# Film block: 21 of the 100 lags of a causal convolution moved to TensorE, the other 79 on VectorE in two halves in turns

## The reference, cut to what matters

```
x = layernorm(x_text, g_norm_in, b_norm_in)
scale_in, shift_in = jnp.split(c_t @ W_film_in + b_film_in, 2, axis=-1)
x = x * (1.0 + mod_gate * scale_in) + mod_gate * shift_in
y = s4d(x, ...)          # y[:, t] = sum over j <= t of K[:, j] * x[:, t - j], plus x * D_skip
scale_out, shift_out = jnp.split(c_t @ W_film_out + b_film_out, 2, axis=-1)
y = y * (1.0 + mod_gate * scale_out) + mod_gate * shift_out
xt = x_text + y
h = layernorm(xt, g_ffn, b_ffn)
```

## Time and profile before

| | us |
|---|---|
| three runs | 5372.17, 5390.11 (median), 5404.51 |
| profiled execution: its time | 5378.79 |
| profiled execution: its span | 5376.5 |
| busy PE / PEld / DVE / ACT / POOL | 4182.6 / 2777.6 / 3022.1 / 2105.8 / 1545.1 |
| L2454, 100 lags: first start, last end | 4848.9, 4969.6 |
| mean granted clock of TensorE | 0.83 of 2.4 GHz |

### The profile page before, as it was taken

How to read it: one execution, slowest core, us unless ns; L and a number is a source line. 1 busy time by engine, 2 the same in 40 slices (tenths; PEclk the granted TensorE clock), 3 DMA queues, 4 the chain that set the end, 5 groups by cost and what they waited for, 6 DMA issues and landing times. The chain is left out here.

```text
span 5376.5 us, 84862 instructions
## 1 busy us (share of the span) xinstructions
PE 4182.6 (78%) x25870; PEld 2777.6 (52%) x25870; DVE 3022.1 (56%) x4511; ACT 2105.8 (39%) x3190; POOL 1545.1 (29%) x911
## 2 busy tenths in 40 slices
PE   7899999999989887578889999983844344340799
PEld 4588888888745456434445555541522222220455
DVE  3344444454333333345456666557369999968333
ACT  2255555555512231124334544441335555530122
POOL 1266666666500031004310000000325555530000
PEclk8799999999979987689779999786866565655699
DMA  2000000000011103120022222210000000000011
GB/s 81 1 9 18 18 12 15 18 18 18 1 34 50 32 9 84 30 68 2 1 54 62 59 59 61 49 26 0 1 23 25 17 25 25 17 10 0 4 56 44
DMA packets 124597, 152.67 MB, mean 28 GB/s; under 512 B 86912, under 2 KB 110224, under 8 KB 124080
## 3 DMA queue, kind: packets, MB, share of 16 engines
q1 hardware_dynamic: 124208, 147.72, 11.0%
HBM read 109.43 MB, written 2.66 MB: 21 GB/s over the span
## 5 line engine op out<-in xcount | busy, mean ns | idle before, releaser
L980 POOL TENSOR_TENSOR pexp_lo<-arena,pexp_hi 128x800 fp32r<-128x800 f32 x384 | 637.4, 1660 | 434.4 <-POOLq L979 433.1
L2123 DVE TENSOR_REDUCE arena<-ps 100x1 f32<-100x482 f32 (+1 forms) x768 | 490.1, 658 | 270.0 <-DVEq L2110 256.9
L2003 DVE TENSOR_REDUCE arena<-ps 128x1 f32<-128x482 f32 (+3 forms) x624 | 393.2, 657 | 361.1 <-DVEq L1981 347.2
L1287 ACT ACTIVATE arena<-ps 128x800 f32<-128x800 f32 x384 | 322.4, 840 | 495.4 <-ACTq L1285 493.4
L2421 DVE MATCH_REPLACE8 arena<-arena 100x1444 f32<-100x1444 f32 x256 | 421.3, 1660 | 0.0
L3140 PE MATMUL ps<-kst,qs 96*100 96x482 f32 (+1 forms) x768 | 378.3, 495 | 45.7 <-PEq L3094 42.0
L1377 ACT ACTIVATE arena<-ps 128x800 f32<-128x800 f32 x384 | 315.3, 837 | 244.5 <-ACTq L1376 244.0
L926 POOL TENSOR_TENSOR max_diag<-w_const,arena 100x800 fp32r<-100x800 f32 x160 | 247.0, 1543 | 451.9 <-POOLq L924 451.9
L2512 DVE TENSOR_TENSOR arena<-ps,arena 128x400 f32<-128x400 f32 x256 | 147.2, 575 | 339.3 <-DVEq L2511 339.3
L3269 PE MATMUL ps<-w_const,w_cross 100*128 100x100 f32 x192 | 43.2, 380 | 375.4 <-PEq L3266 375.4
L1288 ACT ACTIVATE pexp_hi<-ps 128x800 fp32r<-128x800 f32 x384 | 319.5, 832 | 0.0
(11 more groups left out here) (372 smaller groups left out, 9196.6 us busy)
## 6 DMA issues: line engine op xcount, KB each, us to landing
ctxT<-in_ctxT SPq DMA_DIRECT2D x59, 541.5 KB
kst<-mid SPq DMA_DIRECT2D x128, 180.5 KB, 3.1
ctxk<-in_ctx SPq DMA_DIRECT2D x43, 528.0 KB
chunk<-in_ff_chunks SPq DMA_DIRECT2D x77, 193.0 KB, 2.4
arena<-gate_dram SPq DMA_DIRECT2D x64, 200.0 KB, 3.8
kst<-xn SPq DMA_DIRECT2D x64, 180.5 KB, 2.9
arena<-gate_dram SPq DMA_DIRECT2D x64, 100.0 KB, 2.6
w_cross<-in_ca SPq DMA_DIRECT2D x1, 3728.5 KB, 12.3
```

Of the source, the lines that this page charges most:

```text
L980: own(nc.gpsimd.tensor_tensor(pexp_lo[p % 3][:, :, :], pexp[p % 3], pexp_hi[p % 3][:, :, :], ALU.subtract))
L1287: nc.scalar.activation(pexp[p % 3], of, ACT.Exp, scale=scale).then_inc(s.pexp_ready, 1)
L2003: peak = nc.vector.tensor_reduce(mparts[0:at.stop - at.start, m, c:c + 1], bank(k, z - a, at.stop - at.start), AX.X, ALU.max)
L2123: peak = nc.vector.tensor_reduce(mparts2[:, h, c:c + 1], bank(k, z - a, S), AX.X, ALU.max)
```

## The change

In the film block TensorE computes lags 0 to 20 of the convolution. For each of them ScalarE makes a diagonal matrix once, identity times the column of `kernel_l`, in a new tile `lag_diag` in the arena; these 21 instructions stand between `batch(B - 1, 1, last=True)` and `scale(1, 1)`. After `modulate("film_in")` TensorE waits for VectorE's `stage_pe` and adds up 21 products for each group in bank 4 + g, ahead of `modulate("film_out")` in its order. VectorE does the skip and lags 21 to 99, each in two halves of eight batches in turns with a semaphore for each half, then adds the four banks to `y`.

```
@@ setup @@
+    PE_LAGS = 21
+    lag_diag = shared([128, PE_LAGS, 128])
@@ ScalarE, film_block @@
             batch(B - 1, 1, last=True)
+            for j in range(PE_LAGS):
+                ins = nc.scalar.activation(lag_diag[:, j, :], W("const", "ident"), ACT.Copy, scale=kernel_l[:, j:j + 1])
+            own(ins)
+            act.sem_inc(s.k_diag_ready, 1)
             scale(1, 1)
@@ VectorE, film_block @@
             modulate("film_in", xn)
+            dve.sem_inc(s.stage_pe, 1)
             y = squares
-            nc.vector.tensor_scalar(y[:, :, :], xn[:, :, :], W("tk", "skip"), None, ALU.mult).then_inc(s.dve_done, 1)
-            dve.wait_ge(s.dve_done, 1)
-            dve.sem_inc(s.dve_done, -1)
-            for j in range(S):
-                nc.vector.scalar_tensor_tensor(y[:, :, j:S], xn[:, :, 0:S - j], kernel_l[:, j:j + 1], y[:, :, j:S],
-                                               ALU.mult, ALU.add).then_inc(s.dve_done, 1)
+            halves = [slice(0, B // 2), slice(B // 2, B)]
+            for i, h in enumerate(halves):
+                nc.vector.tensor_scalar(y[:, h, :], xn[:, h, :], W("tk", "skip"), None, ALU.mult).then_inc(done[i], 1)
+            for j in range(PE_LAGS, S):
+                for i, h in enumerate(halves):
+                    finished(i)
+                    nc.vector.scalar_tensor_tensor(y[:, h, j:S], xn[:, h, 0:S - j], kernel_l[:, j:j + 1], y[:, h, j:S],
+                                                   ALU.mult, ALU.add).then_inc(done[i], 1)
+            finished(0)
+            finished(1)
+            for g in range(NG):
+                dve.wait_ge(s.film_full, 1)
+                dve.sem_inc(s.film_full, -1)
+                nc.vector.tensor_tensor(group(y, g), group(y, g), bs(bank(4 + g)), ALU.add).then_inc(s.dve_done, 1)
                 dve.wait_ge(s.dve_done, 1)
                 dve.sem_inc(s.dve_done, -1)
             modulate("film_out", y)
@@ TensorE, film_block @@
             modulate("film_in")
+            pe.wait_ge(s.stage_pe, 1)
+            pe.sem_inc(s.stage_pe, -1)
+            pe.wait_ge(s.k_diag_ready, 1)
+            pe.sem_inc(s.k_diag_ready, -1)
+            for g in range(NG):
+                for j in range(PE_LAGS):
+                    ins = mm(bs(bank(4 + g))[:, :, j:S], lag_diag[:, j, :], xn[:, GB * g:GB * g + GB, 0:S - j],
+                             start=j == 0, stop=j == PE_LAGS - 1, skip_group_check=True)
+                ins.then_inc(s.film_full, 1)
             modulate("film_out")
```

## The result

| | before | after |
|---|---|---|
| median of four executions | 5384.51 us | 5325.74 us |
| lowest, highest | 5372.17, 5404.51 | 5303.69, 5339.99 |
| profiled execution, its time | 5378.79 | 5339.99 |
| its span | 5376.5 | 5338.2 |

The ratio is 0.9884, with a 95% interval of 0.9836 to 0.9932: faster, by 0.7 to 1.6%. (It is the ratio of the means of the four; that of the medians is 0.9891.) Of the repetitions used further down, e1's 5375.71 and 5435.35 and e4's 5927.30 count as slow, being over 1.5% above the fastest execution of their kernel, and all ratios leave them out. I had said 5346, with 5326 to 5372 for 8 in 10. The median is 0.3 us under that range, so the range was wrong, and the question is why. The profiled execution, at 5339.99, is the slowest of the four.

A forecast was written before the change was run, and what follows sets the result against it. VectorE was taken to bound the convolution while TensorE idles. Saving 42.3 us and losing 2.3 gave -40.0, from 5378.79 to 5338.8, carried to the level of four executions, 7.6 higher: 5346 us, with 5326 to 5372 for 8 in 10.

The forecast's parts named there:

- lags 21 to 99 in halves: VectorE's convolution: 158 half lags, each overlapping the one before by 0.09 us, take 74.9 us.
- stretch saved: Convolution on VectorE, skip to film_out: film_out starts at 4927.5 instead of 4969.8, 42.3 us saved.
- TensorE's 168 instructions: Lags 0 to 20 on TensorE: 84 products of two instructions, 30,240 columns, 50.4 us at 2.4 GHz.
- diagonals at the end of the attention: ScalarE ahead of `scale(1, 1)`: 21 diagonals take 6.1 us, so GpSimd starts its sums 2.3 us late.
- B: Rival, VectorE's lags: halves don't overlap, 88.9 us in place of 74.9, time 5360 us; chance 0.13.
- C: Rival, VectorE's lags: each half costs as much as a lag now, 111.0 us, time 5382 us; chance 0.03.
- right on the full level, and leave no gap: TensorE's new products start at 4847.9 at the full clock and end at 4898.3, 25 us of slack.
- D: Rival, convolution: TensorE at 1.2 GHz throughout, its products take 100.8 us, time 5370 us; chance 0.06.
- E: Rival, convolution: TensorE's weight loads aren't hidden, its products take 158 us and bound the kernel, 5428 us; chance 0.04.
- The end moves by the same: End of the attention: GpSimd's two sums keep their 3.58 us, so the end shifts by the 2.3 us delay.
- term added for the level: Whole time: the profiled execution is 7.6 us below the mean of four, 5386.4, so the sum is carried to 5346.
- a dear ScalarE: End of the attention, bound for the diagonals: at 0.52 us each, 10.9 us, they cost 7.1 us.

The follow-up runs named there:

- e1: The changed kernel run again, unedited: median 5347.04 us of 12 executions, ratio 0.9900 to the kernel before.
- e4: The changed kernel with the 21 diagonals behind `scale(1, 1)` instead of ahead of it: median 5335.73 us of six, ratio 0.9891 to the kernel before.
- e2: The kernel before with all 100 lags on VectorE in two halves, no diagonals, nothing on TensorE: median 5357.49 us, ratio 0.9969.
- e7: The changed kernel with VectorE's 79 lags in four parts of four batches instead of two halves: 5319.73 us in one execution.
- e6: The changed kernel with TensorE let go only at VectorE's lag 31, when its clock has fallen: 5317.14 us in one execution.

## Why the prediction was wrong, and where it was right

The steps, as the tails show them:

| step | predicted | measured |
|---|---|---|
| lags 21 to 99 in halves | 74.9 | 74.1 |
| stretch saved | 42.3 | 43.4 |
| TensorE's 168 instructions | 50.4 | 52.6 |
| diagonals at the end of the attention | +2.3 | +2.5 |
| from there to the skip | 0 | +0.9 |
| from film_out on | 0 | -0.5 |
| sum | -40.0 | -40.5 (tail) |

- **VectorE: right.** The fixed cost came from the earlier trace rows and the overlap from rows of other instructions; the overlap held to 0.01 us (0.083 against 0.09). B (88.9) and C (111.0) are refused by the changed kernel's own timeline, and B again by e2 and e7.
The Trainium skill's "VectorE: DVE Perf Modes", section "The DRAIN you can't avoid", says that the next operation waits until the pipe is empty, and adds that one which is not held starts earlier; I had drawn B from the first half alone. This case's trace agrees with the addition: a half here starts 0.083 us before the end of the independent one ahead.
- **TensorE: right in what it led to.** The claim that the products start "right on the full level, and leave no gap" was wrong: they had 3.1 us at the lower one, hidden by 22 us of slack. The film_out products of groups 0 and 1, which the prediction itself moved behind the convolution, were TensorE's last work up to 4849 before; without them it is idle for 5.34 us ahead of the new products, and the level falls as these begin. D failed in e6, and E in the changed kernel: 52.6 / 168 = 0.31 us an instruction, with 0.30 the bare columns at the full clock (30,240 x 1.67 ns / 168).
- **ScalarE: right.** 6.23 us for 21 (6.1), 2.5 us lost (2.3), and e4 shows that the order was the whole cause. "The end moves by the same" missed 0.6 us more behind TensorE's first product, which e4 wins back too. To put this at nothing because ScalarE is only at 39% would have been the mistake to make here.
- **The failed step: "the four known executions have a mean of 5386.4, 7.6 above it. I carry the sum to that level", and with it the range.** The term added for the level was +7.6; 48 executions of the kernel before have a mean of 5380.0, 1.2 above the profiled one, so it should have been about +1, which gives 5340. That is 6.4 of the 20.3 us between 5346 and 5325.74, and 0.5 is the tail; the other 13 are the spread, as far as the runs tell. (The 16 executions of the changed kernel have a mean of 5340.0, 5330.7 without the two longest.) And the range took in the cases (B, D, a dear ScalarE) but hardly the spread of a median of four of the kernel after. Four values drawn from those 16 have a median between 5317 and 5354 in 8 of 10 draws, and below 5326 in 23 of 100; from e1's twelve alone, which don't hold the four that were timed, in 13 of 100. The four gave 5325.74, and 12 more 5347.04. That it fell just outside the range, by 0.3 us, and not just inside, is luck. The mechanism and its size stood; the level of a program with 36 us between its executions was taken for known.

What stays open: why the head's time at 1.2 GHz differs from one execution to the next by up to 113 us with the same instructions. The nine profiles show that it does, in stretches far ahead of the change; none of my runs changed its cause.

## What to carry to other kernels

Cut the profiled execution at the first instruction that the change can reach, and compare tails: here the same kernel's repeat to a few tenths while the whole time spreads by over 1%, so the tail sizes a term and only the spread of repeated executions sizes the range. A chain of in-place VectorE instructions has two prices to attack, the wait for its own result (0.15 us, and 0.08 of overlap, which two independent halves hide) and its elements, of which another engine can take a part; here the second was worth about four times the first (35.2 us of the convolution against 9.5 or 8.2). And work that "another engine does meanwhile" needs its preparation too: look at what that engine's next instruction is holding up, and put the preparation behind it.

## What the runs showed of the hardware that I had not expected

- Dense products of 320 to 400 columns that start at a granted clock of 0.50 had it at 1.00 after 5.2 us (e6), and those of e4 after 6.2; the feed-forward of the earlier trace rows took from 5003.9 to about 5018, with gaps in its products.
- In the changed kernel the level fell after 5 us without a product (1.00 up to 4852, 0.57 in 4853 to 4857), just as the next ones began.
- The same 4114 VectorE instructions ahead of the change took from 4742 to 4794 us in nine profiled executions, at 1453 to 1566 us of the lower TensorE clock.
